# Decoder layer, self-attention stage: normalisation on ScalarE, scores ahead of the turned rows, output projection in three split passes

## The reference

```python
q = x @ Wq + bq; k = x @ Wk + bk; v = x @ Wv + bv      # x is (4, 1024, 512)
# windows of 128 rows, every 64 rows
scores = jnp.einsum('bwid,bwjd->bwij', qw, kw) * scale
attn = jax.nn.softmax(scores, axis=-1)
ow = jnp.einsum('bwij,bwjd->bwid', attn, vw)
# overlapping windows are added and divided by their count
out = out / counts[None, :, None]
return out @ Wo + bo
...
x = _layernorm(x + attention(x))     # (x - mean) / sqrt(var + 1e-5)
```

## Time and profile before

| | |
|---|---|
| median of three runs | 4513.71 us (4509.85 to 4514.88) |
| profiled execution | 4517.81 us, of it 4516.2 from the first to the last instruction |
| busy share of that span | PE 87%, DVE 56%, POOL 45%, ACT 33% |
| mean granted TensorE clock | 0.943 of full speed |
| self-attention stage | begins near 405 us, ends near 888 us |

### The profile page before, as it was taken

One profiled execution on the slowest core, in us unless ns is written; L12 is line 12 of the kernel. 1 busy time (PEld: TensorE's weight loads), 2 busy tenths in 40 slices (PEclk: granted clock), 3 DMA queues, 4 the chain that ended last, 5 costly groups with the idle time before them and its releaser, 6 DMA issues. The chain is left out here.

```text
span 4516.2 us, 61725 instructions
## 1 busy us (share of the span) xinstructions
PE 3909.1 (87%) x20188; PEld 3212.3 (71%) x20188; DVE 2526.9 (56%) x8674; ACT 1494.5 (33%) x2415; POOL 2029.2 (45%) x1411
## 2 busy tenths in 40 slices
PE   7857999768668888887999987959999999999998
PEld 4534778567667778776787776748877877778786
DVE  8824776488888988883655553324433455222222
ACT  3644553356456666663001002311111122111111
POOL 0000211158568777775664240036766765333232
PEclk9978999879889999998999998979999999999999
DMA  3435223310100201001542224331212232000000
GB/s 112 156 138 178 85 87 107 97 40 22 40 27 21 61 12 51 29 14 41 199 144 92 98 107 175 112 114 59 73 57 68 70 98 66 22 20 28 24 22 19
DMA packets 234570, 337.06 MB, mean 75 GB/s; under 512 B 56530, under 2 KB 114802, under 8 KB 230900
## 3 DMA queue, kind: packets, MB, share of 16 engines
q1 hardware_dynamic: 146420, 186.17, 13.2%
q10 hardware_dynamic: 85264, 138.46, 8.9%
q0 software_dynamic: 2560, 8.39, 0.5%
HBM read 220.70 MB, written 112.25 MB: 74 GB/s over the span
## 5 line engine op out<-in xcount | busy, mean ns | idle before, releaser
L1632 PE MATMUL xa_ps_t<-xa_diag,xa_s_buf 128*128 128x128 f32 x4096 | 532.1, 291 | 142.9 <-ACT xa_a L1719 74.8
L2881 POOL TENSOR_TENSOR m_act_hl<-m_g,m_act_hl 128x512 fp32r<-128x512 f32 x256 | 356.4, 1392 | 662.5 <-DVE m_act_hl L3133 662.5
L1632 PEld LDWEIGHTS xa_ps_t<-xa_diag,xa_s_buf 128*128 128x128 f32 x4096 | 518.9, 206 | 164.5 <-issue 81.1
L3133 DVE CAST m_act_hl<-m_g 128x512 fp32r<-128x512 f32 x256 | 138.8, 542 | 847.3 <-ACT m_g L3023 847.3
L1796 DVE MAX8 xa_cand<-xa_s_buf 128x8 f32<-128x64 f32 x4096 | 543.0, 219 | 63.8 <-ACT xa_s_buf L1682 38.1
L3023 ACT ACTIVATE m_g<-m_ps_h,up_b 128x512 f32<-128x512 f32 x256 | 176.1, 688 | 1101.4 <-PE m_ps_h L82 1096.3
L80 PE MATMUL m_ps_h<-m_hT,up_w 128*128 128x512 f32 x1024 | 413.7, 404 | 19.6 <-issue 17.6
L81 PE MATMUL m_ps_h<-m_hT,up_w 128*128 128x512 f32 x1024 | 408.6, 399 | 0.0
L82 PE MATMUL m_ps_h<-m_hT,up_w 128*128 128x512 f32 x1024 | 407.5, 398 | 0.0
L1560 POOL TENSOR_SCALAR xa_s_buf<-xa_s_buf,xa_top 128x1024 f32<-128x1024 f32 x120 | 343.3, 2861 | 141.0 <-ACT xa_prob L1701 141.0
L80 PE MATMUL m_ps_o<-m_w,m_act_hl 128*128 128x512 f32 x1024 | 405.6, 396 | 0.7 <-POOL m_act_hl L2881 0.7
(11 more groups left out here) (384 smaller groups left out, 8297.7 us busy)
## 6 DMA issues: line engine op xcount, KB each, us to landing
at_xk<-in_x_dram SPq DMA_DIRECT2D x128, 128.0 KB, 2.7
spectrum<-df_yo ACTq DMA_DIRECT2D x32, 512.0 KB, 2.8
id_raw<-spectrum SPq DMA_DIRECT2D x32, 512.0 KB, 5.6
m_xt<-x ACTq DMA_DIRECT2D x64, 256.0 KB, 3.7
xa_ks<-kt SPq DMA_DIRECT2D x48, 256.0 KB
xa_raw<-in_ctx_dram SPq DMA_DIRECT2D x32, 384.0 KB, 3.3
tp_awT<-in_ctx_dram SPq DMA_DIRECT2D x11, 768.0 KB, 4.7
kt<-tp_aw SPq DMA_DIRECT2D x4, 2048.0 KB, 6.5
```

The lines of the kernel that those rows point to most:

```text
L1632: last = pe.matmul(ps_t[:, c // 4, c % 4, :], s_buf[:, t % 2, h, k0:k0 + P], diag[:, h, :], start=(h == 0 and c % 4 == 0), stop=(h == HEAD ...
L2881: pool.tensor_tensor(lo, g32[:, :], hi.bitcast(F32), ALU.subtract).then_inc(s_gl, 1)
```

## The change

Five things change, all in the stage's engine programs.

1. The projection uses `mm3`. The weights `w_vo` are split once, at the start, into a high half (ACT) and a low half (DVE), both fp32r, in `vo`. The mix is split in each tile: ACT writes the high half (`s_oh`), and DVE subtracts it from the mix for the low half (`mix_lo`, `s_oc`).
2. The normalised rows are written by ACT (`normalised`), as scale times res plus shift. POOL computes the shift, minus mean times rstd, behind the power; DVE negates the mean. ACT writes x1 of tile i - 1 in tile i, ahead of its copy of the mix.
3. PE makes the scores ahead of turning x1, and turns x ahead of `cross_q`.
4. ACT copies the scores ahead of x1, computes the exponentials ahead of copying x, and issues the stores last in the tile.
5. DVE makes the low half of q behind the attention weights instead of ahead of the second pair.

```diff
         attT = sb("attT", [P, 2, P])
-        oT = sb("oT", [P, DC, P])
+        oT = sb("oT", [P, 2, DC, P], F32R)
+        vo = sb("vo", [P, 2, DC, D], F32R)
         res = sb("res", [P, D])
...
         rstd = sb("rstd", [P, 1])
+        shift = sb("shift", [P, 1])
         x1 = sb("x1", [P, 2, D])
...
         s_o = sem("mix_done")
-        s_oc = sem("mix_copied")
+        s_oh = sem("mix_hi")
+        s_oc = sem("mix_lo")
+        s_vh = sem("projection_hi")
+        s_vl = sem("projection_lo")
         s_y = sem("projected")
...
                 def tile(b, j, first, last):
...
                     pool.wait_ge(s_var, i + 1)
-                    pool.tensor_tensor(rstd[:, :], mv[:, 1:2], neghalf[:, :], ALU.pow).then_inc(s_rstd, 1)
+                    pool.tensor_tensor(rstd[:, :], mv[:, 1:2], neghalf[:, :], ALU.pow)
+                    pool.drain()
+                    pool.tensor_tensor(shift[:, :], mv[:, 0:1], rstd[:, :], ALU.mult).then_inc(s_rstd, 1)
                     if not (isinstance(b, int) and i + 2 >= TILES):
...
                         pe.matmul(ps_d[:, :], e_dn[:, h * P:(h + 1) * P], wc[:, h, :], start=True, stop=True).then_inc(s_d, 1)
-                    if not first:
-                        x1_turned(i - 1, (j + 1) % 2)
                     if not last:
...
                     if not first:
-                        cross_q(i - 1)
+                        x1_turned(i - 1, (j + 1) % 2)
                     if not last and not (isinstance(b, int) and i + 2 >= TILES):
                         x_turned(*after(b, j, 2))
+                    if not first:
+                        cross_q(i - 1)
+                    if first:
+                        pe.wait_ge(s_vl, 1)
                     pe.wait_ge(s_oc, i + 1)
-                    pe.wait_ge(s_x1, i)
+                    pe.wait_ge(s_var, i)
                     for c in range(DC):
-                        done = pe.matmul(ps_y[:, :], oT[:, c, :], w_vo[:, c, :], start=(c == 0), stop=(c == DC - 1))
+                        done = mm3(pe, ps_y[:, :], oT[:, 0, c, :], oT[:, 1, c, :], vo[:, 0, c, :], vo[:, 1, c, :],
+                                   c == 0, c == DC - 1)
                     done.then_inc(s_y, 1)
...
+                def normalised(i, k, stores):
+                    act.wait_ge(s_rstd, i + 1)
+                    act.wait_ge(s_st[k], 16 * stores)
+                    act.activation(x1[:, k, :], res[:, :], ACT.Identity, bias=shift[:, :], scale=rstd[:, :]).then_inc(s_x1, 1)
+
                 def x1_copied(i):
...
                         partners(2 * (i - FIRST))
+                    if not first:
+                        normalised(i - 1, 1 - k, (i - 1) // 2)
                     act.wait_ge(s_o, i + 1)
                     act.wait_ge(s_y, i)
-                    act.activation(oT[:, :, :], ps_o[:, :, :], ACT.Copy).then_inc(s_oc, 1)
+                    act.activation(oT[:, 0, :, :], ps_o[:, :, :], ACT.Copy).then_inc(s_oh, 1)
+                    if not last:
+                        scores_copied(i + 1, 1 - k)
                     if not first:
...
                     if not last:
-                        scores_copied(i + 1, 1 - k)
-                    if not first:
-                        q_hi(i - 1, 1 - k, b * (TPB // 2) + (j - 1) // 2)
-                    if not last:
+                        exponentials(i + 1, 1 - k)
                         if not (isinstance(b, int) and i + 2 >= TILES):
                             x_copied(i + 2, k)
-                        exponentials(i + 1, 1 - k)
                     if not first:
-                        store(i - 1, 1 - k)
+                        q_hi(i - 1, 1 - k, (i - 1) // 2)
                     if 0 <= i - PRODUCT < HC:
...
                         partners(2 * (i - FIRST) + 1)
+                    if not first:
+                        store(i - 1, 1 - k)
...
                 exponentials(0, 0)
+                act.wait_ge(s_w, 16 * 7)
+                act.activation(vo[:, 0, :, :], w_vo[:, :, :], ACT.Copy).then_inc(s_vh, 1)
                 batches(tile)
+                normalised(TILES - 1, 1, TILES // 2 - 1)
                 x1_copied(TILES - 1)
...
+                def mix_lo(i):
+                    dve.wait_ge(s_oh, i + 1)
+                    dve.tensor_tensor(oT[:, 1, :, :], ps_o[:, :, :], oT[:, 0, :, :].bitcast(F32), ALU.subtract).then_inc(s_oc, 1)
+
                 def softmax(i, j, q, rounds):
...
                     dve.drain().then_inc(s_mx, 1)
-                    if rounds:
-                        q_lo(q, j % 2)
                     if FIRST <= i - 2 < LAST:
...
                     dve.drain().then_inc(s_att, 1)
+                    if rounds:
+                        q_lo(q, j % 2)
                 def tile(b, j, first, last):
...
                         row_bias(*after(b, j, 1))
+                        mix_lo(i)
                         if FIRST <= i < LAST:
...
                         softmax(i + 1, (j + 1) % TPB, i - 1, not first)
+                    if last:
+                        mix_lo(i)
                     dve.wait_ge(s_y, i + 1)
                     dve.wait_ge(s_xb, i + 1)
+                    dve.wait_ge(s_x1, i)
                     dve.tensor_tensor(res[:, :], ps_y[:, :], xb[:, k, :], ALU.add)
...
                     dve.drain()
-                    dve.tensor_scalar(mv[:, 1:2], mv[:, 1:2], EPS, None, ALU.add).then_inc(s_var, 1)
-                    dve.wait_ge(s_rstd, i + 1)
-                    dve.wait_ge(s_st[k], 16 * (b * (TPB // 2) + j // 2))
-                    dve.tensor_scalar(x1[:, k, :], res[:, :], mv[:, 0:1], rstd[:, 0:1], ALU.subtract, ALU.mult)\
-                       .then_inc(s_x1, 1)
+                    dve.tensor_scalar(mv[:, 0:1], mv[:, 0:1], -1.0, None, ALU.mult)
+                    dve.tensor_scalar(mv[:, 1:2], mv[:, 1:2], EPS, None, ALU.add)
+                    dve.drain().then_inc(s_var, 1)
...
                 softmax(0, 0, None, False)
+                dve.wait_ge(s_vh, 1)
+                dve.tensor_tensor(vo[:, 1, :, :], w_vo[:, :, :], vo[:, 0, :, :].bitcast(F32), ALU.subtract).then_inc(s_vl, 1)
                 batches(tile)
```

## The result

| | before | after |
|---|---|---|
| median of the timed runs | 4513.09 us (4509.85 to 4514.88) | 4485.05 us (4482.64 to 4491.71) |
| span of the profiled execution | 4516.2 us | 4483.4 us |
| first mix product to the next stage's first instruction | 448.37 us | 423.53 us |

The ratio is 0.9941, 95% interval 0.993 to 0.9952: 28.0 us saved by the medians, where 25.4 were forecast and 4488 was predicted.

The account below looks back on a forecast made before the run. A loop through several engines bounds tiles 1 to 14, PE the later ones. Savings 19.9 and 9.5, less 2.2, 1.05 and 0.8, make 25.4 us: 4488.3 us, own range 4479 to 4497, 4474 to 4502 with rivals.

Parts of the forecast that it names:

- block work: POOL's operations in tiles 2 to 7, growing to two of 2.70 us, hold DVE's pair updates: 2.2 us more lost.
- start: Splitting the projection weights on DVE takes 2.50 us after the first tile's attention; 1.45 was idle, so 1.05 late, once.
- end: In the last tile nothing covers the longer POOL and ACT chain for x1: about 0.8 us lost.
- the loop: Before the change, scores, tT copy, maximum, exponentials, attention, res, statistics, POOL and x1 hold tiles without the product at 13.77 us.
- Projection: Twelve fp32r matmuls 0.233 us apart replace eight passes of 0.43: 2.80 for 3.43, saving PE 0.63 a tile.
- Rival 3: Slower: the twelve projection matmuls each start 0.40 us after the last, projection 4.80, time 4546 us; chance 0.05.
- rival 4: No change: split matmuls start 0.286 us apart, new loop stays near 13.3, 3 us saved, 4511; chance 0.05.
- rival 2: Split matmuls run much faster than the MLP's, loops hold both halves near 12.3 us, 39 saved, 4475; chance 0.04.
- x1 on ACT: Moving x1 frees DVE of 2.08 us; ACT takes 0.8, hidden before the mix product; POOL's drain and multiply add 0.5.
- The new loop: Mix, copy, low half, maxima, exponentials, x copied, queries: 12.28 us, tying with PE's 12.31; 12.35 taken for tiles 1 to 14.
- Rival 1: The new loop costs more: tiles 1 to 14 stay at 12.9 to 13.6 us, time 4496 to 4506; chance 0.14.
- Low half: DVE's added subtraction of the mix takes 0.69 us, reads PSUM and is taken as not held by POOL; upper bound 2.53.

Follow-up runs that it names:

- The two runs with half the change each: Changed kernel with projection back in one float32 pass: 4505.67 us, ratio 0.9985; kernel before with the split projection alone: 4510.98 us, ratio 0.9995.

## Why the prediction was right, and where its terms were off

By terms, in the pair of profiles (measured 24.84 from the first mix, forecast 25.35):

| term | forecast | measured | from |
|---|---|---|---|
| tiles 1 to 14 without block work | 19.9 | 20.5 | sums of 14 intervals, 195.41 and 178.65, less block work |
| tiles 15 to 29 | 9.5 | 9.4 | 207.36 less 197.99 |
| block work | -2.2 | -3.8 | 1.91 before, 5.69 after |
| start | -1.05 | -0.5 | tile 0: 11.62 and 12.12 |
| end | -0.8 | -0.8 | last two tiles to the next stage: 33.98 and 34.77 |

That the sum came within 0.5 is in part luck: block work cost 1.6 more than forecast, the first half and the start gave 1.1 back.

- **What bounds.** Right: the first half by the loop, the second by PE. The two runs with half the change each show it, and how near the two were.
- **Projection.** 2.80 forecast, 2.82 measured, 0.235 a matmul. Rival 3 (0.40) and rival 4 (0.286) fall by this, and rival 2 (much faster) too. The Trainium skill, TensorE: Matmul & The Clock Gate, section Back-to-back issue gap, gives 131 ns for 512 columns; these matmuls do not reach it.
- **x1 on ACT.** 0.81 for 0.8, and hidden as worked out. POOL's drain and multiply end 0.34 behind the power (540.74 to 541.08 in the rows above), for 0.5 assumed.
- **The new loop.** 12.35 forecast and 12.33 to 12.35 measured, but not by the loop: with x copied first nothing changed, and with x1 first on both engines a tile took 12.25. PE binds. Its own sum is that 12.25 (12.31 forecast), and the weight load of the cross product, held until the copy of the turned x1 has ended, adds 0.09, which the prediction did not cost. So the number came out partly by chance. Rival 1 did not occur.
- **Low half.** 0.69 and not held. The Trainium skill, SBUF — State Buffer, section SBUF: two separate sides, expects this of an operation with one input in PSUM, and says of a held one that it is blocked until POOL ends. The trace agrees on the first. The held pair update ended 0.55 after POOL, as forecast from the row of before, and not the full 0.74 that the prediction took from the page for comparison.
- **Block work: the step that was mis-sized.** Forecast 4 in all: 2.9 and 1.1. The lighter tile cost 1.0 (13.36). In the worse one mix to queries grew by 2.95 (11.50 against 8.55 in a plain tile), as forecast; the queries to the next mix then grew by 1.74 (5.53 against 3.79). That is the granted clock, which the prediction named as a thing that would make it wrong and did not price.
- **Start.** Sized too high, and not by the split of the weights alone: tile 0 took 11.51 with the split alone and 11.54 with x copied first, which has the split too, against 11.62 before and 11.61 with the projection in one pass. The 0.5 shows only where the split and the copies of x behind the exponentials come together.
- **28.0 or 25.4.** The stage saved 24.8, 23.7 and 23.5 in the three profiles of the changed kernel. The rest of 28.0 can't be put down to the change: the stages behind scatter by more than that, and the second timing of the changed kernel against the one before gave 22.6 (4514.13 less 4491.57).

## What to carry to other kernels

Where one engine's sum and a loop through several engines lie within a few hundredths of each other, as in tiles 15 to 29 here, each half of a change can measure as nothing and both together as a good deal: price both, and do not drop a part because it does nothing alone. When a step is moved on one engine, look at the order of the engine that stands between it and its reader. Look at the weight loads too: a wait that holds the load can be missing in the matmul's row. And a long wait of PE can cost twice: the wait, and what the work behind it takes at a lower clock; cutting a long POOL operation into pieces saved both.

## What was unexpected of the hardware

- The clock fell behind one PE wait of 2.66 us (queries 4.47 instead of 2.84), and at the same tile of four more runs behind waits of 2.19 to 2.61. It stayed at 1.00 where waits of 1.95 and 0.91 had 1.3 of work between them. Behind 1.15 and 1.80 with 0.44 of work between it fell in both runs that have them, to different cost: the last mix took 3.06 in one and 3.78 in the other. What decides it is not settled here.
- A group of matmuls lost 0.09 us though its operand was ready 0.07 ahead of the first matmul. The load of its weights starts 0.11 ahead of that matmul when nothing holds it, and the wait for the operand held the load. The matmul's row shows no wait.
